# Linear attention loop: the scores of the next strip issued ahead of the A·V product of this one

## The reference, cut to what matters

```python
xn  = layernorm(x)                                   # x: (8, 2048, 1024)
q, k = (xn @ Wq.T), (xn @ Wk.T)                      # 16 heads x 16 features
v   = xn @ Wv.T                                      # 16 heads x 64
A   = tril(phi(q) @ phi(k).T)                        # phi = 1, x/2, (x outer x)/(4 sqrt 2)
y   = A @ v                                          # per head
y   = y * rsqrt(mean(y * y) + 1e-5) * g
out = x + y @ Wo.T + W2t @ gelu(W1t @ xn + b1) + b2  # W1t, W2t ternary
```

## Time and profile before

| | us |
|---|---|
| median of the 2 timed runs | 1793.99 |
| the two runs | 1786.11 and 1801.87 |
| the profiled execution, device time | 1767.79 |
| its span on the slowest core (core 5) | 1766.2 |
| spans of the 8 cores | 1742.4 to 1766.2 |
| mean granted TensorE clock of core 5 (1 is 2.4 GHz) | 0.731 |

### The profile page before, as it was taken

One profiled execution on the slowest core, in us unless ns is written; L12 is line 12 of the kernel. 1 busy time (PEld: TensorE's weight loads), 2 busy tenths in 40 slices (PEclk: granted clock), 3 DMA queues, 4 the chain that ended last, 5 costly groups with the idle time before them and its releaser, 6 DMA issues.

```text
span 1766.2 us, 15881 instructions; the slowest of 8 cores (1742.4 to 1766.2 us)
## 1 busy us (share of the span) xinstructions
PE 1106.5 (63%) x4072; PEld 417.8 (24%) x4072; DVE 569.1 (32%) x1295; ACT 533.7 (30%) x886; POOL 93.3 (5%) x154
## 2 busy tenths in 40 slices
PE   0000198576757585757585835918888980599996
PEld 0000043122212121212121211303333330244442
DVE  2222006644444444444444444362222220010000
ACT  2543332343434344434443441203333320000000
POOL 1111000000000000000000001001111110000000
PEclk9999599555555555555555556959999995799998
DMA  9889904100000101010101028744444555465562
GB/s 199 279 282 200 158 1 76 27 1 19 1 18 1 18 1 30 1 30 1 31 1 30 0 48 207 257 166 148 166 155 151 161 165 166 134 163 148 138 167 48
DMA packets 154324, 176.17 MB, mean 100 GB/s; under 512 B 73856, under 2 KB 125056, under 8 KB 150144
## 3 DMA queue, kind: packets, MB, share of 16 engines
q0 software_dynamic: 24928, 97.53, 20.5%
q1 hardware_dynamic: 129312, 77.63, 17.5%
HBM read 119.56 MB, written 41.94 MB: 91 GB/s over the span
## 4 chain that ended last, share of the span: by engine, by line
PE 39%; DMA 32%; DVE 15%; issue 8%; SPq 2%; ACT 1%; POOL 1%; DVEq 1%; POOLq 0%; ACTq 0%
PE psY L737 11%; PE psS L723 10%; DMA wst<-w2T 9%; PE psS L811 6%; DVE pv L442 5%; DMA p1st<-w1T 5%; PE psS L699 5%; DMA hg_ts<-hg_scr 4%; DMA xnT<-xn_tm 4%; DMA w_sb<-w2t_scr 3%; DVE A_buf L457 2%; DMA y_tm<-y_pair 2%; PE psS L775 2%; PE psY L775 2%; PE psY L811 2%
## 5 line engine op out<-in xcount | busy, mean ns | idle before, releaser
L633 ACT ACTIVATE A_buf<-psS,consts 128x512 bf16<-128x512 f32 (+3 forms) x427 | 283.0, 712 | 431.6 <-PE psS L723 430.0
L723 PE MATMUL psS<-qh_ext,kh_ext 16*128 16x512 bf16 (+3 forms) x640 | 268.7, 553 | 113.9 <-DVE A_buf L446 88.3
L737 PE MATMUL psY<-A_buf,v_tm 128*64 128x512 bf16 (+3 forms) x640 | 204.0, 556 | 131.6 <-DVE A_buf L457 130.3
L789 PE MATMUL psS<-xnT,w_sb 128*128 128x512 bf16 x1024 | 228.3, 381 | 73.4 <-DVE w_sb L509 39.3
L442 DVE TENSOR_SCALAR pv<-psS 128x512 bf16<-128x512 f32 (+3 forms) x213 | 129.7, 609 | 240.0 <-PE psS L723 238.7
L811 PE MATMUL psS<-w_sb,hg_ts 128*128 128x512 bf16 x512 | 114.0, 384 | 71.2 <-DMA hg_ts<-hg_scr 71.2
L699 PE MATMUL psS<-xnT,wq_bf 128*128 128x512 bf16 x64 | 21.1, 501 | 209.5 <-DMA xnT<-xn_tm 209.5
L789 PEld LDWEIGHTS psS<-xnT,w_sb 128*128 128x128 bf16 x1024 | 98.1, 98 | 203.4 <-issue 92.9
L737 PEld LDWEIGHTS psY<-A_buf,v_tm 128*64 128x64 bf16 x640 | 82.9, 137 | 250.0 <-issue 237.5
L723 PEld LDWEIGHTS psS<-qh_ext,kh_ext 16*128 16x128 bf16 x640 | 66.6, 118 | 308.6 <-issue 305.6
L666 ACT ACTIVATE hgst<-psS,consts 128x512 bf16<-128x512 f32 x128 | 85.2, 686 | 177.5 <-DMA hg_scr<-hgst 108.8
(11 more groups left out here) (93 smaller groups left out, 642.8 us busy)
## 6 DMA issues: line engine op xcount, KB each, us to landing
p1st<-w1T POOLq DMA_DIRECT2D x16, 1024.0 KB, 6.9
p1st<-w2T POOLq DMA_DIRECT2D x16, 1024.0 KB, 10.1
wst<-w1T POOLq DMA_DIRECT2D x16, 1024.0 KB, 7.9
wst<-w2T POOLq DMA_DIRECT2D x32, 512.0 KB, 4.8
hg_scr<-hgst SPq DMA_DIRECT2D x128, 128.0 KB, 2.5
hg_ts<-hg_scr SPq DMA_DIRECT2D x32, 512.0 KB, 6.5
x_roll<-x SPq DMA_DIRECT2D x16, 512.0 KB, 7.7
out<-out_sb SPq DMA_DIRECT2D x16, 512.0 KB, 4.9
```

The source lines that it names most:

```text
L633: e.activation(A_buf[:, gs % 4, t0:t0 + w], psS[idx % 4][:, 0:w], AF.Square, bias=cc(C_CBI), scale=cc(C_CSC)).then_inc(sPOLY, 1)
L723: e.matmul(psS[idx % 4][:, 0:w], kh_ext[:, hi, m * 128:(m + 1) * 128], qh_ext[:, hi, t0:t0 + w], start=True, stop=True).then_inc(sSC, 1)
L737: mm = e.matmul(psY[64 * hi:64 * hi + 64, t0:t0 + w], v_tm[:, m, h * E:(h + 1) * E], A_buf[:, gs % 4, t0:t0 + w], start=False, stop=False)
L789: mm = e.matmul(ps[:], w12_sb[:, c * FF + j * 128:c * FF + j * 128 + 128], xnT[:, 4 * tb:4 * tb + 4, c, :], start=(c == 0), stop=(c == KD ...
```

## The change

PE's order becomes: scores of strip m, then A·V of strip m-1, then scores of strip m+1, and so on; the A·V of strip 15 and the closing of the last bank come at the pair's end. The closing of a bank moves with the A·V after which it stands. On DVE the copy-out of bank b (now the function `evac_y`) moves behind the polynomials and masks of strip 4b+4; that of bank 3 stays at the pair's end. Waits, semaphores, counts, buffers and every instruction stay as they are, and ACT's, SP's and POOL's code isn't touched.

```diff
+        def evac_y(p, b):
+            e.wait_ge(sCUM, 8 * (4 * b + 4))
+            e.wait_ge(sYB, 4 * p + b + 1)
+            if p > 0 and b == 0:
+                e.wait_ge(sYT, 16 * p)
+            e.scalar_tensor_tensor(
...
@@ vec_stream, at the end of a strip
-                if m % 4 == 3:
-                    b = m // 4
-                    e.wait_ge(sCUM, 8 * (4 * b + 4))
-                    e.wait_ge(sYB, 4 * p + b + 1)
...
+                if m >= 4 and m % 4 == 0:
+                    evac_y(p, m // 4 - 1)
+            evac_y(p, 3)
@@ ten_stream, ahead of the pairs: two functions
+        def emit_av(e, p, m):
+            chs = strip_chunks(m)
+            for hi, h in ((0, 2 * p), (1, 2 * p + 1)):
+                gs = strip_of[(p, m, hi)]
+                for ci, (t0, w) in enumerate(chs):
+                    idx = poly_idx[(p, m, hi, ci)]
+                    if ci == 0:
+                        e.wait_ge(sDM, dm_of[(p, m, hi)] + 1)
...
+                    e.matmul(psY[64 * hi:64 * hi + 64, t0:t0 + w],
...
+                e.sem_inc(sAV, 1)
+
+        def close_b(e, p, b):
...
@@ ten_stream, behind the scores of strip m
-                for hi, h in ((0, 2 * p), (1, 2 * p + 1)):
-                    gs = strip_of[(p, m, hi)]
...
-                if m % 4 == 3:
-                    b = m // 4
...
+                if m > 0:
+                    emit_av(e, p, m - 1)
+                    if (m - 1) % 4 == 3:
+                        close_b(e, p, (m - 1) // 4)
+            emit_av(e, p, NT - 1)
+            close_b(e, p, 3)
```

More of the change, by code:

```diff
@@ L420, in rms_vec2 @@
                                 ALU.mult).then_inc(sRMc, 1)
+        def evac_y(p, b):
[4 more added lines that the diff above has]
+            e.scalar_tensor_tensor(
+                blk(y_pair[:, 512 * b:512 * (b + 1)], 4),
+                vTc[:, 4 * b:4 * b + 4, p, :],
+                0.5, blk(psY[:, 512 * b:512 * (b + 1)], 4),
+                ALU.mult, ALU.add).then_inc(sYE, 1)
         for p in range(8):
@@ L703, in ten_stream @@
         e.wait_ge(sCUM, 8)
+        def emit_av(e, p, m):
[6 more added lines that the diff above has]
+                        e.wait_ge(sDM, dm_of[(p, m, hi)] + 1)
+                    elif owner[idx] == "S":
+                        e.wait_ge(sPOLY, cntS[idx])
+                    else:
+                        e.wait_ge(sPOLYV, cntV[idx])
+                    e.matmul(psY[64 * hi:64 * hi + 64, t0:t0 + w],
+                             v_tm[:, m, h * E:(h + 1) * E],
+                             A_buf[:, gs % 4, t0:t0 + w],
+                             start=False, stop=False)
+                e.sem_inc(sAV, 1)
+        def close_b(e, p, b):
+            e.matmul(psY[:, 512 * b:512 * (b + 1)], zrow_bf[:],
+                     vTc[0:1, 0, 0:4, :], start=False,
+                     stop=True).then_inc(sYB, 1)
         for p in range(8):
@@ L726, in ten_stream @@
                                  start=True, stop=True).then_inc(sSC, 1)
-                for hi, h in ((0, 2 * p), (1, 2 * p + 1)):
-                    gs = strip_of[(p, m, hi)]
[L729 to L741, removed]
-                if m % 4 == 3:
-                    b = m // 4
-                    e.matmul(psY[:, 512 * b:512 * (b + 1)], zrow_bf[:],
-                             vTc[0:1, 0, 0:4, :], start=False,
-                             stop=True).then_inc(sYB, 1)
+                if m > 0:
[4 more added lines that the diff above has]
+            close_b(e, p, 3)
         e.wait_ge(sPOLY, N_CH_S)
```

## The result

The changed kernel takes **1592.19 us** (median of 11 runs, 1587.52 to 1610.97), where the kernel before takes 1771.79 (median of 10 runs, the two shown before the prediction among them). The ratio is 0.8991, with a 95% interval of 0.8951 to 0.903: faster by a tenth. In some executions the cores of one die show a lower granted clock and take some per cent longer; the ratios in this document leave those out, the medians do not. Forecast were 1670 us and a range from 1628. The direction and the place were right, the size was not: the profiled execution fell from 1767.8 to 1587.5, by 180 us, where the sum said 115.

The account below looks back on a forecast made before the run. PE's serial hand-overs, not a full engine, were taken to bound the attention loop. 155.5 - 17.9 - 8 - 8 - 7 = 114.6 us off the profiled 1767.8 gave 1653, plus 18 about 1670 us; range 1628 to 1722.

Parts of the forecast that it names:

- the sum: Attention loop: 155.5 us of empty slots less 17.9, 8, 8 and 7 gives 114.6 us gained.
- The bound: Attention loop: no engine is full; serial order of scores, wait, A·V, next scores on PE costs 130.3 us in 126 waits.
- 155.5 us of empty slots, less 17.9 of hand-over: Before A·V: 130.3 us idle plus 126 x 0.20 goes; 128 hand-overs of 0.14 us remain.
- A·V stays as long as it was: Loop's matmuls: nothing is removed, only the place differs; PE's 490 busy us carried over unchanged.
- Charges of 8, 8 and 7 us: Losses: masks unready on strips 13 to 15, banks at strips 0 and 1, copy-out delaying polynomials at 3 places a pair.
- Pair boundary unchanged: Between pairs: 4.9 us for loading kh_ext and qh_ext, and 7.80 us of waiting at the fifth score, stay.
- The clock stays at 1.2 GHz: Attention loop: TensorE stays at clock 0.50 though busy about 81% of the loop in place of 68%.
- Rival A: Long strips: the clock rises with denser PE work, another 90 us off, about 1580; chance 0.08.
- Rivals B and C: Loop: PE waits for score banks instead, 1775, chance 0.10; DVE's copy-out wait stalls PE, 1830, chance 0.03.
- The offset: Whole kernel: timed runs lay 18 and 34 us above the profiled execution; the nearer, +18, was added to 1653.
- The range: Whole kernel: 1628 to 1722 us, from forecast-case gains of 60 to 137 us and some of the clock-rise case.
- The signs given for it: Loop: mask wait below 25 us, some 600 us long, bank waits 88 to 105, clock 0.50, a pair some 75.

## Why the prediction was right in kind and wrong in size

- **The bound.** Right: PE's queue order set the loop, not a full engine. The 130.3 us of waits before A·V left without a successor.
- **155.5 us of empty slots, less 17.9 of hand-over.** Right: 154.2 by the starts of the matmuls, and 17.6 remain. Adding 0.20 us a wait for the late modelled end was needed; the bare 130.3 would have been 24 short. The 0.14 us of a hand-over was partly luck. The prediction took the last score of strip 7 for one of 128 columns, but a strip's short chunk comes first: by the individual record that score has 512 columns and starts at 370.91, so its slot ends at 371.33 and that hand-over is 0.09 us. The mean of the 120 in the changed kernel is 0.15.
- **A·V stays as long as it was: the step that failed.** The prediction said that nothing is removed and only the place differs, and carried PE's 490 busy us, A·V's 204 among them, into the new loop without a term. By slots A·V fell from 180.3 to 137.4, and PE's busy time to 437. The merged row of six A·V in the earlier trace rows held the hint: 1.99 us by the record, for six matmuls whose slots alone are 2.56, so the heads overlapped, and only partly. I read that row's length and not what it was made of, and did not ask what an instruction's own wait costs when its engine has nothing queued. What the runs showed in its place: with the sequencer held back A·V is at 177.9 again, in the same order. This is 43 of the 62 us that the loop was short of.
- **Charges of 8, 8 and 7 us** for unready masks, for banks after strip 0 and for the copy-out. All too high. Mask waits are 5.8 us and lie within the 17.6; runs of scores grew by 2.3 us in all (strip 1's stall went from 0.43 to 0.74 us); the copy-out cost nothing, as the DVE half alone showed too. Together some 20 us.
- **Pair boundary unchanged.** Right: 7.72 us at the fifth score against 7.80, 24.5 us for kh_ext against 23.6.
- **The clock stays at 1.2 GHz.** Right, and now with a full PE: 10.00 of 10.00 us busy at 0.50. Rival A fell.
- **Rivals B and C** fell: waits for banks 87.2 against 88.3, DVE's wait for the closing down to 24.9 us.
- **The offset.** I added 18 us for the two timed runs above the profiled one. With ten runs the median before is 1771.79, 4 above it. Some 12 of the 78 us between forecast and median come from there, and 65 from the sum: two runs were a poor base.
- **The range** reached 137 us of gain, which was the wait with every charge at zero, so it excluded by construction that work itself becomes shorter. It had no bound for the term I had set to zero. The signs given for it show the same: the mask wait came out as said, but the loop is 541 us and not some 600, a pair 68 and not 75.

## What to carry to other kernels

Issuing the next block's independent matmuls ahead of a waiting product paid twice here: the wait was covered (137 us), and the product's matmuls were queued when their turn came, so those that write different halves of PSUM's partitions ran side by side (43 us). When instructions on one engine each carry their own wait, look at how a block starts after a stall, and order matmuls that could overlap by turns. In a budget, write down also the terms that the change is supposed to leave alone, with a range.

## What the runs showed that I had not expected

- Matmuls that use 64 columns of the array each and write different halves of PSUM's partitions overlap almost fully once both are queued: in strip 4 of the changed kernel the starts are 0.01 us apart, with 0.427 us a slot. How much of that a kernel gets depends on the queue: 180, 146, 137 and 127 us for the same 640 A·V matmuls, by order alone. Their slots one after another are 232 us, so full overlap would be 116 (an estimate from the slots).
- A matmul can even start ahead of one that stands before it in program order. In strip 3 of pair 0 of the kernel before, head 1's first (128 columns, fifth in the program's order) starts at 352.51, and head 0's last (fourth) at 352.81. Where the width of the short chunk tells the heads apart (72 strips), head 1 overtakes so in 38 strips of the kernel before and in 69 of the changed one.
- With the scores on partitions 32 to 47, the first score of strips 5, 9 and 13 in odd pairs (12 cases a core, on all eight) started within 0.004 us of the closing matmul, which reads one row at partition 0; with both at partition 0 the distance was 0.40 us each time (24 of 24 in the changed kernel). So matmuls whose operands lie on different partitions can overlap too.
- PE raises sAV from its sequencer, not at the end of the matmuls ahead of it: in strip 1 of pair 1, core 0, the increment for head 0 was issued at 398.28 and recorded at 398.35, and the strip's first A·V started at 398.48. By the code that is harmless here, since the next writer of the slot also waits for scores that PE issues after that A·V.
